# Four attention layers with routed experts: the projections of a slot in another order, and layer 4's elementwise work shared out differently

## What is computed

```python
x = layernorm(attn(q=x, kv=ctx; mask) @ w_out + b_out + x)       # L0
x = layernorm(relu(x @ w_ff1 + b_ff1) @ w_ff2 + b_ff2 + x)       # L0, feed-forward of 1024
x = layernorm(x + attn(q=x, kv=ctx) @ Wo)                        # L1
x = layernorm(x + attn(q=x, kv=x, causal) @ sa_wo + sa_bo)       # L2
x = layernorm(x + attn(q=x, kv=ctx) @ ca_wo + ca_bo)
x = layernorm(x + moe(x))            # 8 experts of 1024, the best 2 of each token
a = attn(q=x, kv=ctx with one shared key/value head, window of 64 to each side) @ Wo + bo   # L3
g = silu([a, x] @ Wg + bg)
o = a * g + x * (1 - g)
y = o * rsqrt(mean(o * o) + eps) * rms_w
out = y - mean over the tokens of y
```

## Time and profile before

| | us |
|---|---|
| median of three runs | 2612.47 |
| the profiled execution | 2615.38 |
| its span, first to last instruction | 2613.5 |
| stage A, first to last slot's maxima | 1516 (128 slots) |
| stage B, with the transition | 1587 to 2105 |
| stage C, first to last slot's maxima | 445.9 (31 steps) |

### The profile page before, as it was taken

How to read it: one execution, slowest core, us unless ns; L and a number is a source line. 1 busy time by engine, 2 the same in 40 slices (tenths; PEclk the granted TensorE clock), 3 DMA queues, 4 the chain that set the end, 5 groups by cost and what they waited for, 6 DMA issues and landing times. The chain is left out here.

```text
span 2613.5 us, 78679 instructions
## 1 busy us (share of the span) xinstructions
PE 2343.6 (90%) x29712; PEld 1922.1 (74%) x29713; DVE 1579.9 (60%) x3628; ACT 1050.1 (40%) x2612; POOL 917.6 (35%) x1158
## 2 busy tenths in 40 slices
PE   6899899899899899899899977999999968888897
PEld 4777677777677677677677766999999946666665
DVE  4676676676676676676676663111111138888887
ACT  2344344244343344343343334555555523333332
POOL 3344354354354354354453443000000024444442
PEclk9999999999999999999999998999999979999998
DMA  9200000000000000000000006111111111111110
GB/s 216 79 3 26 2 20 25 2 20 24 2 21 24 6 19 22 6 19 22 7 18 6 10 34 216 42 36 36 36 36 36 36 47 42 46 44 46 40 46 21
DMA packets 84506, 93.92 MB, mean 36 GB/s; under 512 B 23296, under 2 KB 75680, under 8 KB 84128
## 3 DMA queue, kind: packets, MB, share of 16 engines
q1 hardware_dynamic: 74432, 63.00, 8.1%
q0 software_dynamic: 9440, 27.29, 3.3%
q10 hardware_dynamic: 384, 0.01, 0.0%
HBM read 62.21 MB, written 28.05 MB: 35 GB/s over the span
## 5 line engine op out<-in xcount | busy, mean ns | idle before, releaser
L1326 DVE TENSOR_REDUCE mb<-ps_scores 128x8 bf16<-128x1024 f32 x320 | 377.3, 1219 | 97.2 <-PE ps_scores L756 94.9
L1709 POOL TENSOR_TENSOR qbd_all<-qT,consts 128x512 fp32r<-128x512 f32 x160 | 168.9, 1055 | 721.0 <-ACT kT L1106 319.5
L1335 DVE RECIPROCAL rs<-ps_o 128x256 f32<-128x256 f32 x160 | 280.7, 1754 | 45.5 <-PE ps_o L811 42.3
L1120 ACT ACTIVATE pt_all<-ps_scores 128x512 f32<-128x512 f32 x512 | 264.0, 604 | 79.4 <-PE ps_scores L784 79.4
L964 PEld LDWEIGHTS ps_scores<-tiles,w_now 128*128 128x128 f32 x2272 | 266.1, 193 | 5.7 <-ACT w_now L1191 1.3
L964 PE MATMUL ps_scores<-tiles,w_now 128*128 128x128 f32 x2272 | 266.7, 276 | 1.5 <-ACT w_now L1191 0.9
L974 PE MATMUL ps_w<-arena,tiles 128*128 x1136 | 257.0, 379 | 2.5 <-ACT tiles L1199 2.5
L1199 ACT ACTIVATE tiles<-ps_scores,b1s 128x128 f32<-128x128 f32 x568 | 154.2, 383 | 233.1 <-PE ps_w L974 230.9
L1815 POOL DMA_INDIRECT arena<-sorted_y,pidx x64 | 62.9, 983 | 495.0 <-DMA sorted_y<-tiles 478.4
L974 PEld LDWEIGHTS ps_w<-arena,tiles 128*128 128x128 f32 x1136 | 210.3, 190 | 28.6 <-issue 2.9
L1732 POOL TENSOR_TENSOR rstd<-ve,neghalf 128x1 f32<-128x1 f32 x192 | 106.1, 553 | 353.4 <-DVE ve L1346 291.6
(11 more groups left out here) (235 smaller groups left out, 4882.2 us busy)
## 6 DMA issues: line engine op xcount, KB each, us to landing
tiles<-sorted_x SPq DMA_DIRECT2D x72, 128.0 KB, 2.0
sorted_y<-tiles SPq DMA_DIRECT2D x71, 128.0 KB, 1.7
cin<-in_ctx SPq DMA_DIRECT2D x48, 128.0 KB, 2.1
w_experts<-in_L_xattn_e_w SPq DMA_DIRECT2D x6, 1024.0 KB, 12.3
arena<-in_L_xattn_e_w POOLq DMA_DIRECT2D x12, 384.0 KB, 3.9
x_scratch<-x2b_all SPq DMA_DIRECT2D x32, 128.0 KB, 1.7
arena<-x_scratch SPq DMA_DIRECT2D x32, 128.0 KB, 2.0
out<-arena SPq DMA_DIRECT2D x32, 128.0 KB, 2.3
```

The costliest lines, as they stand in the source:

```text
L1120: nc.scalar.activation(pt[:, 4 * g:4 * g + 4, :].rearrange("p h q -> p (h q)"), ps_s[:, g, :], ACT.Exp, bias=bias, scale=LAYER[l]["scale"] ...
L1326: last = V.tensor_reduce(mb[:].rearrange("p (g r) -> p g r", g=BANKS)[:, 2 * half:2 * half + 2, 0:SLOTS], ps_s[:, 2 * half:2 * half + 2, : ...
L1335: V.reciprocal(rs[:], ps_o[:, 2:4, :]).then_inc(recip_ready, 1)
L1709: G.tensor_tensor(qbd[p].bitcast(F32R), qT[:].unsqueeze(2).to_broadcast([P, KC, PAIR, P]), hmask.unsqueeze(1).unsqueeze(3).to_broadcast([P ...
```

## The change

1. In stage A `project_v` and `project_qk` become one function, `project`. It waits for `mt_sb` before anything else. Then come keys, values, queries for l = 1, 3 and 4; values, keys, queries for l = 2; values, then queries and keys for l = 0. The wait for `xT` stands behind the keys of l = 1, 3, 4.
2. In the feed-forward slots `project(nxt)` now stands ahead of `wo(prev)`; in the last of them (slot 6) `xt(nxt)` also stands ahead of `scores_t(now)`. DVE's `residual_sum` moves behind `vz_evac` and the router's pieces, still ahead of `qk_lo`.
3. The transposed context `cT` of layer 0 is stored to device memory (SP, 32 stores in stage A) and loaded back in stage C, in place of the load of `ctx`, its transposes on PE and their copy on ACT.
4. In stage C, DVE no longer copies indices (ACT does, three of them ahead of the first slot), copies no weights (the two products read `w_all` directly), takes no mean of squares (ACT: `Square` with accumulation, then the epsilon), and copies neither the attention's output nor the final result out of PSUM (ACT, behind the exponentials, ahead of `mean_square` and the copy of `atT`). The bias `L3_xattn_bo` is folded into others once before the stage, and the mean's matmul becomes identity minus 1/128, so that its result needs no subtraction. POOL's `c_residual` gets a third operation. `GATE`, the steps of DVE's gate counted by a semaphore, goes from 7 to 5.

The diff, cut:

```diff
-        def project_v(n, first_l):
+        def project(n, first_l):
...
-            kv = xT[n["s"]] if l == 2 else cT[n["s"]]
+            wait(pe, mt_sb, t)
+
+            def keys():
+                if l == 4:
+                    wait(pe, ct_loaded[n["s"]], 16 * (n["j"] + 1))
...
+            if l in (1, 3, 4):
+                keys()
             wait(pe, xt_sb, t + 1)
...
             last.then_inc(v_psum, 1)
...
+                if l == 2:
+                    keys()
                 wq = w3q if l == 4 else w_attn[l][0]
                 for o in range(KC):
                     for c in range(KC):
...
                 av(prev)
                 if ff["l"] == 0:
                     fxt(ff, 2)
-                scores_t(now)
+                    scores_t(now)
                 xt(nxt)
+                if ff["l"] != 0:
+                    scores_t(now)
+                project(nxt, first and nxt["s"] == 0)
                 wo(prev, False, w_free)
-                project_v(nxt, first and nxt["s"] == 0)
-                project_qk(nxt)
...
@@ stage A, DVE, feed-forward slots
                 normalise(prev)
-                residual_sum()
                 vz_evac(nxt)
                 router_pieces()
+                residual_sum()
                 qk_lo(nxt)
...
@@ stage A, SP
+            m = at_(0)
+            if m["ok"] and m["l"] == 0:
+                b = m["j"] * NS + m["s"]
+                wait_apart(sp, ctxt_sb, b + 1)
+                sp.dma_start(ct_dram[bass.ds(b, 1)].rearrange("o s d -> s (o d)"),
+                             cT[m["s"]][:].rearrange("p c q -> p (c q)")).then_inc(ct_stored[m["s"]], 16)
...
@@ stage C, SP
-            sp.dma_start(cin[par], a["ctx"][bass.ds(b, 1)].rearrange("o s d -> s (o d)")).then_inc(ctx_loaded[par], 16)
+            wait_apart(sp, qk_psum, NT + b - NS + 1)
+            sp.dma_start(cT[s][:].rearrange("p c q -> p (c q)"), ct_dram[bass.ds(b, 1)].rearrange("o s d -> s (o d)")).then_inc(ct_loaded[s], 16)
...
@@ stage C, PE
-            mm(ps_w[:, D:2 * D], mean_w[:].to_broadcast([P, P]), xh[n["p"]], start=True, stop=True).then_inc(c_mean, 1)
+            mm(ps_w[:, D:2 * D], centre, xh[n["p"]], start=True, stop=True).then_inc(c_mean, 1)
...
-            if nxt["ok"]:
-                ctxt(nxt)
...
@@ stage C, ACT
+        def index_prep(n):
+            b = n["b"]
+            wait(act, c_gathered[n["p"]], 32 * n["h"])
+            nc.scalar.copy(pidx[n["p"]][:], pos_all[:, bass.ds(b * TOPK, TOPK)]).then_inc(c_idx, 1)
+
+        def mean_square(n):
+
+            b = n["b"]
+            wait(act, c_gstep, GATE * b + GATE)
+            nc.scalar.activation(sq, go, ACT.Square, scale=float(D) ** -0.5, accum_out=ssq[:]).then_inc(c_sq, 1)
+            wait(act, c_sq, b + 1)
+            nc.scalar.activation(ve[3][:], ssq[:], ACT.Identity, bias=eps_col).then_inc(c_ve, 1)
+
+        def finish(n):
+            b = n["b"]
+            wait(act, c_mean, b + 1)
+            wait(act, c_out[n["p"]], 16 * n["h"])
+            nc.scalar.copy(fin[n["p"]], ps_w[:, D:2 * D]).then_inc(c_fin, 1)
+
+        act.wait_ge(table_step, TABLE_POS)
+        act.wait_ge(c_prep, 3)
...
             if now["ok"]:
                 exps(now)
+            if prev["ok"]:
+                wait(act, wo_ready, prev["t"] + 1)
+            if m_["ok"]:
+                finish(m_)
+            if prev["ok"]:
+                nc.scalar.copy(at[prev["s"]], ps_w[:, 0:D]).then_inc(c_at, 1)
+            if h_["ok"]:
+                mean_square(h_)
             if g_["ok"]:
                 wait(act, c_att_psum, g_["b"] + 1)
                 nc.scalar.copy(atT, ps_xv[:, 0:D].rearrange("p (c q) -> p c q", c=KC)).then_inc(c_att_sb, 1)
...
@@ stage C, DVE
-            V.tensor_copy(wsel[p][:], w_all[:, bass.ds(b * TOPK, TOPK)])
-            V.tensor_copy(rsm[:, 0:1], zeros[:, 0:1]).then_inc(rt_w_step, 1)
...
-            gate_link(n, 6, V.scalar_tensor_tensor(gd, go, 1.0 / D, go, ALU.mult, ALU.mult, accum_out=ssq[:]))
-            gate_link(n, 7, V.tensor_scalar_add(ve[3][:], ssq[:], RMS_EPS))
...
-            if prev["ok"]:
-                wait(dve, wo_ready, prev["t"] + 1)
-            if m_["ok"]:
-                finish(m_)
-            if prev["ok"]:
-                V.tensor_tensor(at[prev["s"]], ps_w[:, 0:D], row3["L3_xattn_bo"][:], ALU.add).then_inc(c_at, 1)
             if nn["ok"]:
                 combine(nn)
```

More of the change, by code:

```diff
@@ L201, in program @@
     fin = [cv([D]) for _ in range(2)]
+    xrb = [cv([D]) for _ in range(NS)]
+    ln3_b_bo, centre = cv([D]), cv([P])
+    sq, eps_col = cv([D]), cv([1])
     with nc.sbuf_tensor("w1_now", [P, 2, KC, FF], F32) as w1_now:
@@ L376, in program @@
     mask_loaded = [sem(f"mask_loaded{i}") for i in range(NS)]
+    ct_stored = [sem(f"ct_stored{i}") for i in range(NS)]
+    ct_loaded = [sem(f"ct_loaded{i}") for i in range(NS)]
     x2_stored = [sem(f"x2_stored{i}") for i in range(NS)]
@@ L604, in store_c @@
             sp.dma_start(out[bass.ds(b, 1)].rearrange("o s d -> s (o d)"), fin[par]).then_inc(c_out[par], 16)
-        load_c(0, 0)
-        load_c(1, 1)
-        load_c(2, 0)
+        for s in range(NS):
+            sp.wait_ge(ct_stored[s], 16 * ITERS)
+        load_c(0, 0, 0)
+        load_c(1, 1, 1)
+        load_c(2, 0, 2)
         def run_c(j, st, b, first, last):
@@ L701, in project_v @@
             last.then_inc(v_psum, 1)
-        def project_qk(n):
-            t, l = n["t"], n["l"]
-            src = xT[n["s"]]
-            kv = src if l == 2 else cT[n["s"]]
-            wait(pe, mt_sb, t)
             if l == 0:
@@ L902, in run @@
                 xt(now)
-                project_v(now, True)
-                project_qk(now)
+                project(now, True)
             if now["ok"]:
@@ L933, in run @@
                 if nxt["ok"]:
-                    project_v(nxt, first and nxt["s"] == 0 and nxt["l"] > 0)
-                    project_qk(nxt)
+                    project(nxt, first and nxt["s"] == 0 and nxt["l"] > 0)
                 if now["ok"]:
@@ L1021, in mean @@
             wait(pe, c_gstep, GATE * (b + 1) + 1 if n["ahead"] else GATE * b + 1)
-            mm(ps_w[:, D:2 * D], mean_w[:].to_broadcast([P, P]), xh[n["p"]], start=True, stop=True).then_inc(c_mean, 1)
+            mm(ps_w[:, D:2 * D], centre, xh[n["p"]], start=True, stop=True).then_inc(c_mean, 1)
         pe.wait_ge(ld_l3, 16 * 11)
+        pe.wait_ge(b_y, TILES + 1)
+        for c in range(KC):
+            last = mm(ps_w[:, 0:D], col["L3_xattn_bo"][:, c:c + 1].to_broadcast([P, P]), w3g[:, c, :], start=c == 0, stop=c == KC - 1)
+        last.then_inc(c_bo_psum, 1)
+        pe.wait_ge(c_prep, 3)
         def run_c(j, st, b, first, last):
@@ L1034, in run_c @@
                 pe.wait_ge(b_y, TILES)
-                ctxt(now)
                 xt(now)
-                project_v(now, False)
-                project_qk(now)
+                project(now, False)
             if now["ok"]:
@@ L1207, in _ @@
         act.wait_ge(ld_w1, 16 * W1_EARLY)
+        for s in range(NS):
+            act.wait_ge(ct_stored[s], 16 * ITERS)
         copy_weights(0, 0)
```

107 lines of the change are left out of this document (49 added, 58 removed).

## The result

| | us |
|---|---|
| before, median of four runs | 2613.93 (2605.62 to 2616.98) |
| after, median of four runs | 2573.02 (2572.03 to 2579.32) |
| ratio after / before | 0.9848, 95% interval 0.9819 to 0.9876 |
| the profiled execution of after, its span | 2572.03, 2570.2 |

The change makes the kernel 1.5% faster. Between the two profiled executions the difference is 2572.03 - 2615.38 = -43.3 us. By stage, taken between the same maxima in both traces: stage A 1515.7 -> 1532.1 (**+16.5**), the stretch from stage A's end to stage C's first maxima 589.8 -> 590.0 (+0.2), stage C 445.9 -> 382.7 (**-63.3**), what follows the last maxima 37.1 -> 40.4 (+3.3).

A forecast was written before the change was run, and what follows sets the result against it. It took PE to bound stage A and DVE stage C. Terms -38 + 48 - 43 - 1 = -34 gave 2581 against the profiled 2615.4; less 3 to the median, 2578 us, own range 2560 to 2599, 8 in 10 2545 to 2610.

The forecast's parts named there:

- feed-forward slots: Stage A, slots 3 to 6: PE's waits shrink, 4.7 us an iteration, times 8: -38 us, bounds -20 to -50.
- plain slots: Stage A: the projection's wait for mt_sb adds 0.51 us in each of 95 slots: +48 us, bounds +34 to +61.
- stage C: PE becomes the bound; slots fall from 14.4 to 13.0 us over 31 slots: -43 us, bounds -62 to -18.
- lead-in: Start of stage C: earlier gathers and one copy less, but the bias passes PE and DVE first: -1 us, -4 to +3.
- tail: Kernel's end: five hops a slot stay more or less equal, 0 us.
- The first projection starts near 751.2, 0.51 later: Plain slots of stage A: nothing covers ACT's copy of the maxima, so the first projection waits 0.51 us more.
- the sum adds 0.42: 1.24 earlier: Slot 4: values come 1.66 us earlier, residual_sum ahead of qk_lo costs 0.42, so ff_hidden's second half gains 1.24.
- some half-clock time will stay, 0.2 us a slot: Stage C: some half-clock time remains while PE is the bound, raising the slot from 12.8 to 13.0 us.
- Rival 1: Stage C: ACT reaches atT in time, the gate's new wait doesn't show; 12.4 us a slot, 2559 us; chance 0.15.
- Rival 2: Stage A: the wait for mt_sb costs little, the path regains it; -38 alone, 2530 us; chance 0.08.
- Rival 3: Stage C stays bound by DVE through the port lock with POOL; 13.9 us a slot, -16, 2605 us; chance 0.17.
- Rival 4: Plain slots of stage A: PE's added idle time drops the clock to half; +56, 2634 us; chance 0.10.

The follow-up runs named there:

- e3: The kernel before with only the feed-forward slots' new order; plain slots and stage C as before: ratio 0.9799, 2560.4 us.
- e2: The kernel before with one wait moved: stage A's values also wait for mt_sb: ratio 1.0277, 2682.9 us.
- e1: The changed kernel with values ahead of the mt_sb wait, keys behind it, in stage A's plain slots: ratio 0.9604 to before, 2506.7 us.
- e7: The changed kernel with stage C's two copies out of PSUM and their wait for wo back on DVE: ratio 0.9987 to before, 2611.1 us.
- e8: The changed kernel with stage C's keys back behind the queries: ratio 0.9928 to before, 2591.6 us.
- e4: The changed kernel with ACT's copy of atT ahead of the mean of squares in stage C: ratio 0.9887 to before, 2579.1 us.
- e9: Stage A in before's order, except keys ahead of queries and cT stores kept; stage C as changed: ratio 0.9812 to before, 2557.0 us.
- e6: e4 with POOL's two gathers in a slot of stage C moved behind expand_lo: ratio 0.9885 to before, 2580.6 us.

## Why the prediction was right, and where it was not

The forecast was 2578 us, and the median is 2573.02. Faster, and in the range, by the mechanisms named. But three terms were too small, by 16 to 21 us each, and they do not have the same sign: that the sum is within 5 us is in part luck. Against the profiled execution, for which it gave 2581, it is 9 us off.

| term | forecast | measured | without the clock |
|---|---|---|---|
| feed-forward slots | -38 | -55.2 (e3) | -33 |
| plain slots | +48 | +64.2 (e2), +68.7 (after less e1) | +56, +53 |
| stage A | +10 | +16.5 | +18 |
| stage C | -43 | -63.3 | |
| lead-in | -1 | +0.2 | |
| tail | 0 | +3.3 | |
| sum | -34 | -43.3 | |

- **Plain slots.** "The first projection starts near 751.2, 0.51 later": it started 0.51 later in after (0.58 behind L807 in place of 0.07) and 0.60 in e2, and a slot got 0.56 to 0.59 longer. The wait at the next scores stayed at 0.33, as argued. The step is right; the term misses some 0.07 us a slot and the clock. (Its upper bound of +61 comes to +63 by its own working, 95 x (0.51 + 0.15).)
- **Feed-forward slots.** Slot 3 (1.0): 1.1. Slot 5 (1.24): 1.2. Slot 6 with the scores behind it: 4.6, of which 3.4 us are a half-clock stretch of 6.8 us that is gone, leaving 1.2. Slot 4 (1.24): **0.5**. The step that failed there is "the sum adds 0.42: 1.24 earlier". It took the router's pieces at their old durations, though they were to start 1.66 us earlier against POOL's work, and they stretched by 0.6 us more than before.
- **The clock in stage A** was in no term of the sum. Half-clock stretches are read in the earlier trace rows itself: 0.72 us for 16 scores, which take 0.43 to 0.52 at full clock. I quoted that row for its wait and passed over its duration. e3 takes 44 of 51 us away (-22 us). With both parts together they come back in slots 4 and 8: after has 47.6 us. So -55 and +64 do not just add to 9; the slot-by-slot parts without the clock, -33 and +53 to +56, less 2 for the clock, make 18 to 21, against 16.5 measured.
- **Stage C** was 12.34 us a slot, not 13.0. The chain on PE was right: 12.54 in a steady slot less the gate's wait of 0.37 (10.4 us over 28 slots) is 12.17, against 12.23 forecast. The gate's wait was put at 0.55 (0.50 by the prediction's own times, 2328.05 - 2327.55), some 5 us of the 20 missed. The step that failed is "some half-clock time will stay, 0.2 us a slot": none stayed, 6 us. The start of the stage, where samples are not yet gated, has two slots of 10.0 us, which a flat 31 slots passed over: 2 x 2.5 = 5 us. Of the 63.3 us gained, e7 gives back 36.3 (two copies and a wait) and e8 15.2 (the keys' place); the transposes and the load of `ctx`, the index copies, the copied weights and the mean of squares were not run apart, and nothing shows that the parts simply add.
- **Rival 1** (the gate's wait doesn't show): it shows, 10.4 us. e4 took it away and stage C became 9.2 us longer.
- **Rival 2** (the wait for `mt_sb` costs little): false, by e1 and e2.
- **Rival 3** (stage C stays with DVE by the shared port): false for after, true for e7, which has two copies more on DVE and is no faster than before. The prediction said that the stretch would move to the products of `combine`; in after it misses them (487 and 507 ns) and is at L1678 (1013 ns), where DVE has room, in e4 and e7 it hits one of them. With the lock of the Trainium skill, SBUF — State Buffer, section "SBUF: two separate sides", the trace agrees in one point: the stretched instruction ends only behind POOL's (e4: 2388.56 and 2388.26). In another it differs, see the last section: the section gives the ports to whichever operation starts first.
- **Rival 4** (the clock falls in plain slots): in its mild form it is part of the truth. e2 has 17 us more at half clock than before, not 112; the fall in after comes in slots 4 and 8, 3.4 us each.

What stays open: what the 3.3 us of the tail are, and why after has its half-clock stretch in slot 4 of each steady iteration and e1 does not, with the same wait of 2.15 us ahead of the same matmuls. e9 shows that the wait alone does not decide it. A run that shifts an iteration without changing its waits was not tried. In e4 and e6, that the collisions are the cause of the longer slots is argued from which instructions stretched and from PE's waits for DVE, and so is that the gate's wait kept them apart in after; a run without POOL's work in that place was not tried. Half of the half-clock time is its price in stage A (e9), where PE sets the pace. In stage C, where DVE does, e3 has 13.6 us less of it than before and is only 2.9 us shorter.
